# Eight instead of four steps of the fifth chunk's shared expert ahead of the routed blocks

## The reference

```python
def _swiglu(x, w1, w2, w3):
    return jax.nn.silu(x @ w1) * (x @ w2) @ w3
shared_out = _swiglu(x, shared_w1, shared_w2, shared_w3)      # width 256 -> 1024 -> 256
scores = jax.nn.sigmoid(x @ router_w)                         # 16 experts
_, top_idx = jax.lax.top_k(scores + expert_bias, 2)
...
acc + _swiglu(xf, w1, w2, w3) * g[:, None]                    # each routed expert: 256 -> 256 -> 256
...
x = x + jnp.tanh(g_ffn[0]) * (shared_out + routed_out)        # of layer-normed x
```

## Time and profile before

| | us |
|---|---|
| median of 3 runs | 559.43 |
| lowest and highest | 558.39, 563.18 |
| the profiled execution, in all | 562.16 |
| its span, first to last instruction | 560.4 |

### The profile page before, as it was taken

One profiled execution on the slowest core, in us unless ns is written; L12 is line 12 of the kernel. 1 busy time (PEld: TensorE's weight loads), 2 busy tenths in 40 slices (PEclk: granted clock), 3 DMA queues, 4 the chain that ended last, 5 costly groups with the idle time before them and its releaser, 6 DMA issues.

```text
span 560.4 us, 13037 instructions
## 1 busy us (share of the span) xinstructions
PE 533.4 (95%) x4164; PEld 346.6 (62%) x4164; DVE 401.7 (72%) x896; ACT 307.7 (55%) x592; POOL 248.8 (44%) x242
## 2 busy tenths in 40 slices
PE   5998999999899999994999999999999999999997
PEld 2566778565565656662666666666666656566564
DVE  0276798957987777772888888888888647677775
ACT  3424777683246566640777777777777733233332
POOL 3000332335147777875444433444443045666770
PEclk9969899999999999997999999999999999999999
DMA  7996576639206020102233333333344122374442
GB/s 184 308 381 225 180 231 228 211 130 316 76 0 208 8 89 0 39 0 60 80 111 109 110 100 103 114 105 105 100 108 100 58 90 80 96 243 128 138 142 83
DMA packets 53437, 72.55 MB, mean 129 GB/s; under 512 B 8049, under 2 KB 43441, under 8 KB 53377
## 3 DMA queue, kind: packets, MB, share of 16 engines
q1 hardware_dynamic: 44192, 51.75, 28.5%
q0 software_dynamic: 8608, 17.91, 11.6%
q10 hardware_dynamic: 576, 2.10, 1.1%
HBM read 49.64 MB, written 22.09 MB: 128 GB/s over the span
## 4 chain that ended last, share of the span: by engine, by line
PE 69%; POOL 13%; DVE 6%; issue 5%; DMA 4%; ACT 2%; SPq 1%; DVEq 0%; ACTq 0%; POOLq 0%
PE bank L1480 17%; PE bank L1576 17%; POOL slot_token L551 13%; PE bank L1501 9%; PE bank L1602 8%; PE bank L1586 4%; PE bank L1560 3%; DMA X<-in_x 3%; PE bank L1375 2%; PE bank L1341 2%; PE bank L1355 1%; PE bank L1363 1%; PE bank L1345 1%; PE bank L1388 1%; ACT WR L623 1%
## 5 line engine op out<-in xcount | busy, mean ns | idle before, releaser
L1480 PE MATMUL bank<-XTC,WS 128*128 128x512 f16 x768 | 176.3, 379 | 1.6 <-DVE WS L927 1.0
L1480 PEld LDWEIGHTS bank<-XTC,WS 128*128 128x128 f16 x768 | 74.7, 98 | 80.4 <-DVE WS L927 1.3
L568 POOL DMA_INDIRECT ROWS<-xrow,idx x72 | 77.2, 1073 | 96.2 <-PE bank L1560 82.8
L1576 PE MATMUL bank<-WR,XTB 128*64 x432 | 100.2, 381 | 0.5 <-DVE STAGE L1223 0.4
L1576 PE MATMUL bank<-STAGE,XTB 128*64 128x512 f16 x432 | 100.2, 381 | 0.0
L585 POOL DMA_INDIRECT ROWS<-yrow,posi x64 | 63.8, 997 | 55.0 <-DMA yrow<-ROWS 26.8
L551 POOL DMA_INDIRECT slot_token<-tokid,sloti x64 | 72.2, 1129 | 34.9 <-issue 19.2
L795 ACT ACTIVATE STAGE<-WR 128x1024 f16 x72 | 76.8, 1066 | 18.5 <-PE bank L1602 17.9
L717 ACT ACTIVATE SIL<-bank 128x512 f32<-128x512 f32 x63 | 37.6, 597 | 81.9 <-PE bank L1480 80.7
L1576 PEld LDWEIGHTS bank<-WR,XTB 128*64 128x64 f16 x432 | 44.7, 110 | 43.7 <-issue 7.2
L1115 DVE SCALAR_TENSOR_TENSOR G<-bank,SIL 128x512 f32<-128x512 f32 x63 | 43.4, 689 | 28.9 <-ACT SIL L717 28.2
(11 more groups left out here) (171 smaller groups left out, 853.2 us busy)
## 6 DMA issues: line engine op xcount, KB each, us to landing
WR<-in_routed_w SPq DMA_DIRECT2D x39, 256.0 KB, 4.4
yrow<-ROWS SPq DMA_DIRECT2D x72, 128.0 KB, 1.7
X<-in_x SPq DMA_DIRECT2D x4, 1024.0 KB, 14.4
xrow<-STAGE SPq DMA_DIRECT2D x8, 512.0 KB, 4.9
xtd<-STAGE SPq DMA_DIRECT2D x8, 512.0 KB, 3.0
out<-X SPq DMA_DIRECT2D x7, 512.0 KB, 3.1
WR<-in_shared_w SPq DMA_DIRECT2D x3, 1024.0 KB, 12.9
WR<-in_ctx_t SPq DMA_DIRECT2D x3, 768.0 KB, 10.3
```

The costliest lines, as they stand in the source:

```text
L568: pool.indirect_dma_start(out=XG[:, u, :], out_offset=None, in_=xrow, in_offset=bass.IndirectOffsetOnAxis(ap=idx[:, b:b + 1].bitcast(U32), ...
L1480: last = pe.matmul(acc[:, :], WS[:, wx, at:at + P], XTC[:, u, xx, k, :], start=(k == 0 and m == 0), stop=(k == KD - 1 and m == 2))
L1576: last = pe.matmul(bank[u][part, :], XTB[:, b % 4, xx, k, part], w[s], start=(k == 0 and m == 0), stop=(k == KD - 1 and m == 2), tile_posi ...
```

## The change

All 8 steps of chunk 4 now run ahead of the blocks: NSE is 40, the chunk is added once, based(c) is c + 1, and the accumulation flags no longer have a case for the split. The 32 halves of weights are spread over 40 steps instead of 36. ACT issues the load of chunk 6 at step 39, and SP keeps the load of chunk 7. The routed additions begin at step NSE + 3 = 43 and are spread over 20 steps. At the second seam the two steps between the last blocks' rows are 40 and 41.

```diff
-        EX = 4
-        NSE = NSA + EX
+        NSE = NSA + J
 
         def based(c):
 
-            return c + 1 if c < NCA else c + 2
-
-        CUTS = [0] * (J + 5) + [2, 1] * 10 + [1] * 2 + [0]
+            return c + 1
+
+        CUTS = [0] * (J + 5) + [2, 1] * 6 + [1] * 14 + [0]
         assert len(CUTS) == NSE and sum(CUTS) == 2 * E
-        FIRST, LEFT = NSE + 4, NC * J - 1 - (NSE + 4)
+        FIRST, LEFT = NSE + 3, NC * J - 1 - (NSE + 3)
         TILES = {FIRST + q: (q + 1) * NT // LEFT - q * NT // LEFT for q in range(LEFT)}
...
-            for u in range(2):
-                sp.wait_ge(s_h, (NCA + 1 + u) * J)
-                sp.dma_start(XTC[:, u, :, :, :].rearrange("p a k n -> p (a k n)"),
-                             xtd[(NC - 2 + u) * P:(NC - 1 + u) * P, :]).then_inc(ld_xtc[u], 16)
+            sp.wait_ge(s_h, (NC - 2) * J)
+            sp.dma_start(XTC[:, LAST % 2, :, :, :].rearrange("p a k n -> p (a k n)"),
+                         xtd[LAST * P:NC * P, :]).then_inc(ld_xtc[LAST % 2], 16)
...
-            def add_shared(c, combined=None, steps=J):
-                dve.wait_ge(s_y, c * J + steps)
+            def add_shared(c, combined=None):
+                dve.wait_ge(s_y, c * J + J)
...
-            add_shared(NCA, steps=EX)
+            add_shared(NCA)
...
-                if n % J == 1:
+                if n % J == 1 and n // J - 1 > NCA:
                     add_shared(n // J - 1, combined=2 * done)
...
-                                         start=(n in (NSE, n - j) and m == 0 and i % 2 == 0),
-                                         stop=((j == J - 1 or n == NSE - 1) and m == 2),
+                                         start=(j == 0 and m == 0 and i % 2 == 0),
+                                         stop=(j == J - 1 and m == 2),
...
-            hidden(NSE, NCA % 2, EX)
+            hidden(NSE, (NCA + 1) % 2, 0, load=(NCA + 1) // 2 * 16 + 16)
             block_rows(NRUN - 2, es[NRUN - 2 - LAST_WORD])
-            hidden(NSE + 1, NCA % 2, EX + 1)
+            hidden(NSE + 1, (NCA + 1) % 2, 1)
```

## The result

The changed kernel takes 557.37 us (median of 20 runs), the kernel before took 560.99 over 20 runs beside it. The ratio is 0.9934 with a 95% interval of 0.9912 to 0.9957: 3.7 us less (2.4 to 4.9), where 6.1 were forecast. The direction was right, the size was not. 557.37 us lies at the upper end of the stated range. Of its distance to the forecast 553.3 us, 1.6 us come from the base, since the forecast was taken off a median of 3 runs (559.43) where 20 runs gave 560.99; the other 2.4 us are gain that did not come. Medians here are over all runs, while ratios and intervals leave out those in a slower state (2 of these 20 with the change), so a ratio can differ a little from that of two medians.

A forecast was written before the change was run, and what follows sets the result against it. TensorE was taken as the bound except at the first seam, where GpSimd is last. Seam -9.4 and end +3.3 sum to -6.1 us, off the 559.43 us median: 553.3 us, range 549.8 to 557.4.

The forecast's parts named there:

- The seam's gain, 9.4 us: At the first seam: the 7.94 us wait goes, plus 1.45 us from the low clock behind it, 9.4 us in all.
- The moved steps at 3.90 us: Ahead of the blocks: four shared steps moved there take 3.90 us each, 15.6 us of TensorE.
- rival (D): Ahead of the blocks: the four moved steps stall, taking back half the 7.94 us hole; 557.3 us, chance 0.05.
- GpSimd behind TensorE in the last stage: Last stage: VectorE asks for tiles faster than gathers deliver; the last gather delays the end, TensorE standing some 3.3 us.
- Rival (A): Last stage: GpSimd stays hidden, needing 1.26 us a gather, so the gain is the seam's 9.4; 550.0 us, chance 0.15.
- The first gather "stays at 455.18" behind the last block's store: Start of last stage: the first gather waits for that store, so on the old trace's times it stays at 455.18.
- The end term: End of last stage: the last gather's tile makes VectorE late, so TensorE stands 3.3 us before the last 12 matmuls.
- The gathers' rate, 1.31 us: Last stage: GpSimd's gathers without slot waits take 1.31 us each, between 1.293 and 1.344.
- rival (B): Last stage: GpSimd slows to 1.43 us a gather, the end moves 7.6 us; 560.9 us, chance 0.05.
- TensorE bears that: Last stage: VectorE's stands of up to 2.3 us don't hold TensorE, since gate products are needed 3.7 us later.
- What slows a gather: Last stage: the rest of a gate product holds GpSimd's gathers back (1.42 us instead of 0.95), additions don't.
- rival (C): Last stage: additions hold gathers back too, 0.37 of them by 0.24 us on average, 5.6 us; 558.9 us, chance 0.05.

## Why the prediction was wrong in its size

- **What bounds the kernel; the hole.** Right. The wait of 7.94 us is gone, the clock at the seam is 1.00, the down projection there takes 1.48 us with its pipelined end where it took 2.56.
- **The seam's gain, 9.4 us.** Measured 9.10 with eight steps and 9.56 with six (17.73 - 8.17). With eight, TensorE waits 0.87 us for VectorE at the transposes before the first regular pair, with six 0.58. What makes VectorE 0.3 us later there wasn't settled. (The working had a slip of its own: 3.69 - 2.19 is 1.50 us, not 1.45.)
- **The moved steps at 3.90 us.** Right: 15.45 us for four. No stand ahead of the blocks, rival (D) falls.
- **GpSimd behind TensorE in the last stage.** Right as a mechanism: no slot waits, VectorE waits for gathers, the end moves with the last one. One gather a tile removes it. Rival (A) falls, although the profiled span of 551.1 looks like it: what makes that span is a front part 3.8 us shorter.
- **The first gather "stays at 455.18" behind the last block's store.** This step failed. I took the distance from the last block to the first gather as fixed. It grew from 2.7 to 4.1 to 4.7 us, because the code load then fell on the store. The end term hangs on this start: with the load moved off the store by 80 increments the stands are 2.67 us, with the load back on it by 256 they are 4.53. From the first step on the kernel with 80 gained 6.08 us, where 6.1 were forecast. Term by term: the seam gave 9.10 (forecast 9.4), the end cost 15.6 - 12.2 = 3.4 (3.3), the four steps took 15.4 (15.6), and the blocks ran 0.15 us shorter; that these small misses cancel is luck.
- **The gathers' rate, 1.31 us.** The traces show 1.29 and 1.31 (81.31 and 82.70 in 63 intervals). Right; rival (B), with 1.43, falls. In the first trace the faster rate nearly made up for the late start, so its stands of 3.08 us are near the forecast's 3.3 by luck.
- **"TensorE bears that."** Wrong for two steps in the stage. I checked the gate products only, which have 3.7 us to spare. The down projections of steps 48 and 56 wait for a shared addition that stands behind the gathered tiles in VectorE's queue, and have less. Stands of 0.7 to 2.6 us appear there. They do not add to the sum, since a stand early in the stage makes the last one shorter: the run without stores had 5.5 us in three places, that with four steps behind 5.6 in two.
- **The end term, 3.3 us.** The term that was mis-sized. The last stage, four steps or 15.6 us shorter, should have lost 3.3 of them; in the two traces of the changed kernel it lost 15.6 - 11.8 = 3.8 and 15.6 - 9.9 = 5.7. There were stands of 3.1, 4.9, 5.6 and 5.5 us in four traces with eight steps ahead, and 5.0 us by the runs with and without the second gather. The size follows the last gather. By the forecast it starts 537.7 - 452.53 = 85.2 us after the stage's first step and costs 3.3. In the traces with two gathers a tile it starts after 85.0 us (stands of 2.67, with 80 increments), 85.5 (3.08), 87.0 (4.53, with 256), 87.2 (5.46, without stores), 87.4 (4.86) and 88.0 (5.60, four steps behind). Another 0.4 us lies behind it: the last additions start 1.30 us after the last down projection (545.56 to 546.86) and not 0.93. That is so in all kernels with eight steps, one gather a tile included, and its cause stays open.
- **What slows a gather.** Read too much from one row. Gathers that start inside a gate product (one operand in SBUF) took 0.95 or 0.96 us, all 163 of them in the twelve traces. Of those that start inside additions some took up to 1.26, as at 522.22 above, inside additions from 522.17 on. The trace of before had such a row too, in the second of two additions that run from 539.87 to 540.86:

```profile
540.48 1.21 POOL L585 DMA_INDIRECT ROWS<-yrow,posi  x1 [0.30 <-issue]
```

  So the additions hold gathers back as well. The row at 486.52 is no exception. It merges four additions, and the gather began 0.13 us before the end of one of them. In rests and additions alike, all gathers that were longer than usual took 0.95 us plus what was left of the VectorE instruction at their start less 0.13 us, within 0.01 us; with 0.14 us or less left, or when they began in the first 0.03 us of a rest or in some cases in the first 0.09 us of an addition, they kept their 0.95. In the first trace of the changed kernel 20 gathers began in a routed addition and took 1.035 us on average: 0.08 us more, and not 0.24 as rival (C) had it. The rule of the Trainium skill (SBUF — State Buffer, "Who interferes with whom"), that a VectorE instruction with two SBUF inputs contends with a GpSimd instruction that reads SBUF, speaks of both, and here the traces agree with it. The total barely shows it, as fewer gathers now meet a rest: their busy time is 63.05 and 64.46 us against 63.80.
- **The range.** Its upper end as added up, 553.3 + 2.1 + 0.6 + 1.25, is 557.3 us and not 557.4. That the changed kernel's median lies there is chance. None of the three additions was seen in the changed kernel's traces: the gathers took 1.29 and 1.31 us and not 1.344, their landings 2.8 and 2.9 us by the median and not 3.5, and the clock at the end was 1.00. (In rival (A) the gathers would have 82.5 - 3.3 = 79.2 us and not 79.6; the 1.26 us each stand.)
- **From span to median.** Taking the sum off the median and not off a span was sound, though the median of 3 runs stood 1.6 us under that of 20. The front part differs from execution to execution whatever the kernel: in these traces its length goes from 100 us at a granted clock of 0.98 to 107 at 0.94, with the same work in it. The profiled execution of before was one of the long ones and the changed kernel's a short one, which is why spans alone would have said 9.3 us.

The best of these kernels has six steps ahead: 552.19 and, with the additions three behind, 551.58 us, ratios of 0.980 and 0.983 to before, against 0.993 for all eight.

## What to carry to other kernels

When work is moved into a hole, move as much as the hole holds: past that, each further step takes cover from whatever the work hid at its old place, and the time goes up again (0.980 with the hole full, 0.993 with two steps more). Not all of that is lost cover. From the first step on six steps take 445.1 us, eight take 449.1 and 450.9, and eight with the code load moved off the store 448.5: some 3.4 us are the price of the two steps, and the code load adds to it, by 2.0 us in the pair made to test it. Before pricing an engine that comes close behind the bound, list every instruction of the bounding engine that waits for something in that engine's queue, not only the frequent one. And compare traces stage by stage from a common event, since a front part that varies by 4 us can hide or double a change of 4.

## What the runs showed of the hardware

- A load of instruction code of one engine delayed another engine's data store: the last of 9 late packets came 1.3 to 1.9 us behind the other 135 in six traces of six, and all that waits for the store with them. Adding 80 instructions on TensorE's queue took the load off this store, adding 256 left it there.
- A semaphore increment on TensorE's queue, with nothing else to do, costs 0.154 us each.
- Holes of 7.94 and 3.98 us left TensorE at a granted clock of 0.50 for 3.58 us and of 0.56 for 3.65; stands of up to 3.3 us in the last stage did not: the last 12 matmuls took 1.47 to 1.49 us in every trace.
